# First expert stage begun inside the last causal attention round, and expert side steps at other slots

## The reference

```python
x = L0_attn_x                                                      # (4, 1024, 128)
x = _layernorm(x + _L0_attn_ref(x, Wqkv, Wout))                    # 16 heads of 8, causal
x = _layernorm(x + _L0_ffn_ref(x, Wg, W1, W2, W3))                 # 8 experts of 256, top 2
x = _layernorm(x + _L1_attn_ref(x, w_qkv, w_out, b_out))           # rope, 16 heads of 8, full
x = _layernorm(x + _L1_ffn_ref(x, rW1, rb1, rW2, rb2, We1, be1, We2, be2))   # 4 experts of 512, top 2

# L0 attention: exp(clip(q.k * SCALE, -10, 10)) under the causal mask, normalised by its row sum
# L0 experts
scores = einsum('bsd,ed->bse', x, Wg)
topk_scores, topk_idx = top_k(scores, 2)
topk_probs = softmax(topk_scores)
hidden = silu(x @ W1[e]) * (x @ W2[e])
out = sum_e gating[e] * (hidden @ W3[e])
# L1 experts: router = gelu(x @ rW1 + rb1) @ rW2 + rb2, softmax, top 2, experts gelu(x @ We1 + be1) @ We2 + be2
```

## Time and profile before

| what | value |
|---|---|
| median of 3 runs | 1613.22 us (1602.71 to 2422.7) |
| profiled execution | 1611.3 us, of which the span from first to last instruction is 1609.5 us |
| TensorE busy | 1471.5 us (91%) |
| VectorE busy | 1400.4 us (87%) |
| ScalarE busy | 1202.9 us (75%) |
| GpSimd busy | 307.5 us (19%) |
| mean granted TensorE clock | 0.952 |
| chain that ended last | PE 61%, DVE 15%, ACT 10%, issue 10% |

### The profile page before, as it was taken

How to read it: one execution, slowest core, us unless ns; L and a number is a source line. 1 busy time by engine, 2 the same in 40 slices (tenths; PEclk the granted TensorE clock), 3 DMA queues, 4 the chain that set the end, 5 groups by cost and what they waited for, 6 DMA issues and landing times.

```text
span 1609.5 us, 32282 instructions
## 1 busy us (share of the span) xinstructions
PE 1471.5 (91%) x11200; PEld 797.1 (50%) x11200; DVE 1400.4 (87%) x2394; ACT 1202.9 (75%) x1897; POOL 307.5 (19%) x325
## 2 busy tenths in 40 slices
PE   7989898689999999969999999999999998999996
PEld 4333333377777777623333333333333334777775
DVE  5899999878888988887999999999999973788886
ACT  4999999644445454417999999999999986777775
POOL 0000000234455454420000000000000001234333
PEclk9899999799999998966999999999999997999999
DMA  6636432131224431111111111111111110211211
GB/s 203 203 106 182 120 102 86 49 107 40 96 93 127 128 108 66 66 41 51 46 37 37 46 45 38 42 37 36 37 36 36 37 32 28 69 56 63 75 56 40
DMA packets 71026, 116.76 MB, mean 73 GB/s; under 512 B 23808, under 2 KB 33920, under 8 KB 70272
## 3 DMA queue, kind: packets, MB, share of 16 engines
q1 hardware_dynamic: 70912, 115.21, 23.5%
HBM read 73.49 MB, written 41.16 MB: 71 GB/s over the span
## 4 chain that ended last, share of the span: by engine, by line
PE 61%; DVE 15%; ACT 10%; issue 10%; POOL 1%; DMA 1%; DVEq 0%; ACTq 0%; SPq 0%; POOLq 0%
PE full_o L718 14%; PE hid_pair L1031 12%; PE max_pair L689 11%; ACT cprobs L491 7%; PE bank L1134 7%; DVE negmax_h L808 5%; PE score L703 4%; PE causal_o L463 3%; PE triple L447 2%; PE bank L1066 2%; ACT o_sb L779 1%; DVE st L1284 1%; PE hid_pair L952 1%; PE bank L1094 1%; DVE hid_lo L1458 1%
## 5 line engine op out<-in xcount | busy, mean ns | idle before, releaser
L771 ACT ACTIVATE probs<-score 128x512 f32<-128x512 f32 x1024 | 546.6, 596 | 89.5 <-PE score L703 69.5
L808 DVE TENSOR_REDUCE negmax_h<-max_pair 128x2 f32<-128x1024 f32 x512 | 588.6, 1216 | 24.9 <-PE max_pair L689 24.8
L718 PE MATMUL full_o<-probs,v_st 128*32 128x256 f32 x4096 | 337.9, 403 | 17.7 <-ACT o_sb L779 17.7
L703 PE MATMUL score<-q_st,k_st 32*128 32x512 f32 x1024 | 319.9, 510 | 2.6 <-ACT probs L771 2.6
L689 PE MATMUL max_pair<-k_st,q_st 32*128 32x512 f32 x1024 | 264.7, 515 | 12.2 <-DVE negmax_h L808 10.8
L491 ACT ACTIVATE cprobs<-triple 128x1536 f32<-128x1536 f32 x192 | 258.4, 1713 | 5.2 <-PE triple L447 5.2
L689 PEld LDWEIGHTS max_pair<-k_st,q_st 32*128 32x128 f32 x1024 | 97.8, 188 | 236.7 <-DVE negmax_h L808 179.9
L1240 ACT ACTIVATE act_s<-hid_pair 128x512 f32<-128x512 f32 x128 | 76.7, 599 | 149.5 <-PE hid_pair L1031 149.5
L1031 PE MATMUL hid_pair<-x_hi,w_hi 128*128 128x512 f32 x384 | 171.3, 446 | 1.8 <-DVE x_lo L1401 1.0
L521 DVE TENSOR_SCALAR cprobs<-cprobs 128x1536 f32<-128x1536 f32 (+6 forms) x272 | 160.7, 618 | 2.9 <-ACT cprobs L491 2.9
L463 PE MATMUL causal_o<-cprobs,v_st 128*32 128x512 f32 (+3 forms) x1536 | 156.2, 502 | 2.2 <-DVE cprobs L521 2.2
(11 more groups left out here) (157 smaller groups left out, 2001.8 us busy)
## 6 DMA issues: line engine op xcount, KB each, us to landing
gate_all<-gate_scr SPq DMA_DIRECT2D x48, 512.0 KB, 4.3
o_scr<-o_sb SPq DMA_DIRECT2D x64, 256.0 KB, 2.1
k_st<-k_scr SPq DMA_DIRECT2D x64, 128.0 KB, 2.8
q_st<-q_scr SPq DMA_DIRECT2D x128, 64.0 KB, 2.5
k_st<-k_scr SPq DMA_DIRECT2D x64, 96.0 KB
q_st<-q_scr SPq DMA_DIRECT2D x64, 96.0 KB
q_scr<-qk_hi SPq DMA_DIRECT2D x18, 256.0 KB, 4.6
k_scr<-qk_hi SPq DMA_DIRECT2D x18, 256.0 KB, 4.5
```

The costliest lines, as they stand in the source:

```text
L703: nc.tensor.matmul(sbank[L.score_bank(e)][:, :], k_st[p][rows, kt * P:(kt + 1) * P], q_st[p][rows, q0:q0 + w], start=True, stop=True, tile ...
L718: last = nc.tensor.matmul(full_o[SLOT * j:SLOT * (j + 1), cols], v_st[p][:, kt, j, :], probs[s % NP][:, j, cols], start=(kt == 0 and part ...
L771: nc.scalar.activation(probs[s % NP][:, L.HEADS[j], :], sbank[L.score_bank(e)][:, :], ACT.Exp, scale=SCALE).then_inc(L.exp_done, 1)
L808: nc.vector.tensor_reduce(negmax_h[:, qt // TPC, half, heads[0]:heads[1] + 1:2, qt % TPC], ring[slot][:, :, :], AXX, ALU.max, negate=True) ...
```

## The change

**What it does.** (1) The last causal round gets a VectorE routine of its own. The first front runs in it: `o_proj` in TensorE's slot 8, statistics and reciprocal at VectorE's slot 9, `norm` at slot 10, `x_turn` at slots 10 and 11. The router, its top 2 and the gate weights follow in the expert stage's first slots, where the first hidden product now stands ahead of the last values of the attention. The division of the first chunk goes to GpSimd, the first front uses PSUM bank 0, and SyncE loads its operands earlier. (2) `w1` and `w2` are rounded in a piece of 512 and one of 1536 columns, `w3`'s rounding follows the first Silu, and its lower part is made in two pieces. (3) GpSimd's fills of `k_st` and `q_st` move to the end of its first chunk, and its additions stand in another order beside `x_lo` and the rope sums. (4) The plan's slots change; in the first experts `norm` goes from 3 to 4, `x_turn` 4 to 6, router 5 to 7, `weigh` 8 to 10, `g_turn` 10 to 13, `norm2` 4 to 6, `x2_turn` 6 to 8, `q` 7 to 9, `k` 8 to 11, `v` 9 to 12. VectorE's reciprocal for the next front stays at 7, in the same slot as the router and ahead of it in the code. In the second experts `x_turn` goes from 6 to 7, the router's first product (`hidden`) 8 to 9, router 11 to 12, `weigh` 13 to 14, the gate transpose 1 to 2.

```diff
@@ plan
-        for pl, steps in ((plan[0], (2, 4, 6, 7, 8, 9, 1, 1, 3, 4, None, 5, 8, 10)),
-                          (plan[1], (5, 7, None, None, None, None, 1, 1, 3, 6, 8, 11, 13, None))):
+        for pl, steps in ((plan[0], (2, 6, 8, 9, 11, 12, 1, 1, 4, 6, None, 7, 10, 13)),
+                          (plan[1], (5, 7, None, None, None, None, 1, 1, 3, 7, 9, 12, 14, None))):
             (pl.y_turn, pl.norm2, pl.x2_turn, pl.q, pl.k, pl.v,
              pl.o_turn, pl.o_proj, pl.norm, pl.x_turn, pl.hidden, pl.router, pl.weigh, pl.g_turn) = steps
-        GATES_AT, WEIGH_AT = 1, 1
+        FRONT_0_PE = {8: (plan[0].o_proj,), 10: (plan[0].x_turn,)}
+        PIECE = 4 * P
+        PIECES = (slice(0, PIECE), slice(PIECE, NH * P))
+        GATES_AT, WEIGH_AT = 2, 1
-    BESIDE_BACK = {1: (0,), 2: (1,), 4: (2, 3), 7: (4,), 8: (5, 6), 9: (7,)}
+    BESIDE_BACK = {1: (0,), 2: (1,), 6: (2, 3), 9: (4,), 11: (5, 6), 12: (7,)}
@@ pe_round, pe_first_hidden
-                pe_slot_values(pe, L, i, p, n)
+                if not nxt:
+                    for step in FRONT_0_PE.get(n, ()):
+                        pe_beside(pe, stages[1], step, None, 0, 0, 0)
+                if nxt or n < L.N - 1:
+                    pe_slot_values(pe, L, i, p, n)
             for n in range(h_lead[layer]):
                 pe_hidden(pe, st, 0, 0, n, layer)
+                if layer == 0 and n == 0:
+                    pe_slot_values(pe, layers[0], NG - 1, 1, layers[0].N - 1)
@@ new in VectorE's program
+        def dve_last_round(dve, L):
+            st, i = stages[1], NG - 1
...
+            for n in range(L.N):
+                if n == 9:
+                    dve_beside(dve, st, plan[0].o_proj, None, 0, 0, 0)
+                    dve_rcp(dve, st, 1)
+                if n == 10:
+                    dve_w_lower(dve, 0)
+                    dve_beside(dve, st, plan[0].norm, None, 0, 0, 0)
+                if n == 11:
+                    dve_beside(dve, st, plan[0].x_turn, None, 0, 0, 0)
+                dve_clip(dve, L, i, n)
...
+        def dve_w_lower(dve, piece):
+            cols = PIECES[piece]
+            for k in range(2):
+                dve.wait_ge(w_upper, 2 * piece + k + 1)
+                nc.vector.tensor_tensor(w_lo[k][:, cols], w_raw[k][:, cols], w_hi[k][:, cols].bitcast(F32),
+                                        ALU.subtract).then_inc(w_lower, 1)
+        def dve_w3_lower(dve, piece):
+            blocks = slice(0, PIECE // P) if piece == 0 else slice(PIECE // P, NH)
+            dve.wait_ge(stages[1].w3_upper, 1)
+            nc.vector.tensor_tensor(w3_lo[:, blocks, :], w3[:, blocks, :], w3_hi[:, blocks, :].bitcast(F32),
+                                    ALU.subtract).then_inc(stages[1].w3_lower, 1)
@@ dve_chunk, first experts
+                    if m == 0:
+                        dve_save_o(dve, layers[0], NG - 1, 1, layers[0].V * NG)
+                        dve_w3_lower(dve, 0)
+                        dve.wait_ge(layers[0].o_kept[1], 16 * NG)
                     if m > 0:
                         dve_lower0(dve, st, m - 1)
                     if m == 1:
+                        dve_beside(dve, st, plan[0].router, None, 0, 0, 0)
+                        dve_w3_lower(dve, 1)
+                    if m == 2:
                         dve_weights(dve, dve_front[0], st, 0, 0)
                         dve_spread(dve_front[0], st)
@@ act_chunk, act_beside, act_end
-                if layer == 0 and n == pl.norm2:
+                if layer == 0 and n == pl.norm2 + 1:
                     act.wait_ge(st.norm2, back + 1)
+                    if c + n == 0:
+                        nc.scalar.activation(w3_hi[:, :, :], w3[:, :, :], ACT.Copy).then_inc(st.w3_upper, 1)
-                    if c == 0 and n == 4:
+                    if c == 0 and n == 5:
                         act_save_gates(act, st, 0)
@@ dve_beside
-                if n == (pl.o_turn - 1 if front == 0 else (7, 10)[layer]):
+                if n == ((pl.o_turn - 1 if front == 0 else 10) if layer == 1 else 7) and (layer == 1 or front > 0):
                     dve_rcp(dve, st, front + 1)
@@ pe_beside, router's first product (second experts); pe_chunk, gates of the first chunk
                     if back is not None:
-                        pe.wait_ge(st.stats2, back + 1)
+                        pe.wait_ge(st.back_chain, back * BACK_LINKS + 1)
-                if n == (2, GATES_AT)[layer] and (layer == 1 or c == 0):
+                if layer == 0 and c == 0 and n == PIECE // P:
+                    pe.wait_ge(st.w3_lower, 2)
+                if n == (3, GATES_AT)[layer] and (layer == 1 or c == 0):
                     pe_turn_gates(pe, st, c)
@@ pool_experts0
+            pool_divide(pool, st, 0)
...
+                if c == 0:
+                    pool_rows(pool, layers[0])
```

110 lines of the change are left out of this document (58 added, 52 removed).

## The result

The changed kernel took **1617.2 us** in the median of 9 runs (1613.7 to 1619.8), the kernel before 1609.2 in 9 runs beside it. The ratio is 1.0063, with a 95% interval of 1.0047 to 1.0080: slower by 0.6%. The profiled execution took 1617.8 us, of which the span is 1616.0, against 1609.5 before. I had forecast 1597, at most 1610. A change of less than 2% either way had a chance of 0.80, and it is one, but slower and outside my range.

A forecast was written before the change was run, and what follows sets the result against it. It took TensorE and VectorE as nearly equally busy in the first experts, with chains of waits elsewhere. 1611.3 - 1.3 (front) - 1.5 (middle chunks) - 1.9 (chunk 6) - 10.0 (second experts) = 1596.6 us, range 1578 to 1610.

The forecast's parts named there:

- The first front: Between attention and first experts: gates 0.7 us earlier, next hidden product about 335.4; net -1.3 us, bounds -8 and +3.
- So `gate_all` lands about when it did, 333 to 334: First front: later gate turn and save cost 1 to 2 us, so the gain ahead becomes a wait.
- The remark on GpSimd's fills: First front: moved fills cost subtractions beside them nothing by the Trainium skill; priced like additions, 1 us worse.
- A middle chunk: First experts: wait for `xs` goes, `x2_turn` waits for `lead`; 0.3 us gained in each of chunks 1 to 5, -1.5.
- one or two more of them fall so: 0.6 to 1.3: Middle chunk: VectorE subtractions newly beside a GpSimd addition, each 1.32 us instead of 0.68, add 0.6 to 1.3 us.
- Chunk 6: First experts: its 48.09 us at clock 0.89 was an accident; it comes out at 46.2, -1.9 us.
- The second experts: Of TensorE's 13.5 us of waits for `xs`, `mv` and `gts`, 3.0 and 0.5 stay: -10.0 us, bounds -13.5 and -5.
- 0 left of 3.7: Second experts: TensorE's 3.7 us of waits for `mv` vanish, the router's first product being a slot later, released by the residual.
- B: Rival, first experts: the longer wait at `x2_turn` drops the clock for long; 1617 us or more, chance 0.10.
- A: Rival, first experts: wait at `x2_turn` under 2 us, clock no longer falls, 43 us a chunk; 1579 us, chance 0.20.
- C: Rival, second experts: the spread brings nothing because `gate_all` is late by as much; 1606 us, chance 0.10.
- D: Rival, first front: it pulls the gates' transfer with it, -8 instead of -1.3; 1590 us, chance 0.10.

The follow-up runs named there:

- lead_only: Changed kernel with x2_turn waiting only for the router scores' copy, and chunk 0's router top 2 moved ahead of the weights' second lower piece; 1599.8 us.
- turn_only: Changed kernel with x2_turn waiting only for the router scores' copy, and the first front's gate weights, turn and save moved earlier; 1600.2 us.
- front_only: Changed kernel with both tables of steps, their waits and copies, GpSimd's order and the gate's slot as before; 1614.6 us, ratio 1.0049.
- second_only: Kernel before with only the second experts' steps spread and the router's first product waiting for the residual; 1601.8 us, ratio 0.9975.
- light_gpsimd: Changed kernel with GpSimd's first-expert additions and x_lo (from the third chunk) cut to 8 of 512 columns, for measuring only; 1581.6 us, ratio 0.9832.
- best_spread_late: Changed kernel with earlier x2_turn, first front's top 2, gate weights, turn and save earlier, GpSimd's first-expert additions waiting for VectorE's subtraction; 1583.9 us, ratio 0.9849.

## Why the prediction was wrong

**The first front: -1.3 forecast, +4.1 measured.** The single steps were right: first hidden product about 306 (307.19), `o_proj` of chunk 1 at 322.4 (321.47), gates 0.7 us earlier (0.4). The step that failed is "So `gate_all` lands about when it did, 333 to 334"; it went on at 336.15, and the hidden product that I put at 335.4 started at 337.59. I gave the later turn and save 1 to 2 us; the save came 2.6 later and `gate_all` 3.1. The turn stood behind `o_proj` of chunk 1, which the late division held, and then behind two slots of products, in part at 1.2 GHz. lead_only and turn_only show both causes, 4.2 and 5.9 us. front_only had 2.3 of the 4.1 us; in the changed kernel TensorE ran 6.8 us at 1.2 GHz from 319.8 on, in front_only 3.4, which by estimate is up to 1.7 of the rest (`gate_all` let go at 334.96 there, 1.2 us before the changed kernel). The remark on GpSimd's fills was right, see below.

**A middle chunk: -0.3 forecast, +2.6 measured in the mean.** The mechanism was the one I named: no wait for `xs`, one wait on `lead` of 3.6 to 4.2 us (4.16), a wait of 0.6 for `v` (0.41). The term mis-sized is "one or two more of them fall so: 0.6 to 1.3". It was three more, 2.2 us in all: 2.9 ahead of `lead` against 0.7. With 2.2 in place of it my sum is 2.4 + 0.6 + 0.54 - 1.56 + 2.2 = 4.2 us, and `lead` came (442.02 - 419.87) - (429.76 - 412.23) = 4.6 later. `x2_turn` came (442.33 - 419.87) - (430.24 - 412.23) = 4.5 later; less the 4.16 of the slots behind it, with my 0.9 for the clock and 0.4 for `v`, that is a loss of 1.6, and this chunk grew by 1.8. The mean of 2.6 also holds two chunks of 49.4 and 49.5 us, the last with 6.8 us at 1.2 GHz, that I did not follow further. The rest of the step was careless: 4.16 us of slots less 3.3, less 0.9 for the clock and 0.6 for `v`, is a loss of 0.6 and at best a gain of 0.1, but I wrote "0 to 1.5" and took a gain of 0.3. The bound, a loss of 0.7 us a chunk, was too near as well. The Trainium skill (page "SBUF — State Buffer", section "SBUF: two separate sides") has the port pair that VectorE and GpSimd share as an exclusive lock for the whole instruction; by that I had counted three waiting subtractions ahead of `lead`, and the trace agrees with the lock: 1.41, 1.76 and 1.38 us where 0.68 is usual. I had put it beside the sum and not in it.

**Chunk 6** came out of its 10 us at 1.2 GHz, but to 47.5 us and not to 46.2: -0.6 in place of -1.9. **Full attention** I had left to chance; its stretch of the table gave 6.2 us. The stretch at 1.2 GHz at its start was 51 us long in the profile of before, of which my window of 28 us showed a part only, so the term was larger than the 10 us I wrote, and it hid a part of the loss in the total.

**The second experts: -10.0 forecast, -4.7 measured, -6.2 in second_only.** "0 left of 3.7" for `mv` held. The whole idle time of TensorE in a steady chunk fell from 30.28 - 28.30 = 1.98 to 29.13 - 28.29 = 0.84 us, 1.1 and not my 10.0 / 6 = 1.7. The wait for `gts` kept 1.7 us in all and not 0.5. What I missed is the divided tile: the reciprocal kept its slot while the chunk grew shorter, and its load came late in the last chunks, 1.5 and 1.0 us.

**The rivals.** B's 1617 us is what was measured, and that is luck: its own sum is 1611.3 - 11.3 + 20.4 - 1.9 = 1618.5, and its clock of 0.89 in several chunks did not come. It named the place of the loss but not its mechanism: the clock did not fall for long after the wait (3.4 us in most chunks, 0.96). A was near a kernel without GpSimd's traffic: 43.1 us is what light_gpsimd's chunk took, and 44.2 one of best_spread_late. C did not happen as told: VectorE waited for `gate_all` twice there, 1.4 us in all. D needed the gates first: then the front pulls the transfer with it, by 8 us.
